# Decoder layer, attention output: twelve TensorE transposes and two ScalarE copies per step replaced by one DMA transpose

## The reference

```
_, o = jax.lax.scan(step, S0, xs)                    # per head: state 96 x 192, output 192 wide
gate = (hidden_states @ Wg).reshape(B, T, H, DV)     # H = 16, DV = 192
var = jnp.mean(o * o, axis=-1, keepdims=True)
o = o * jax.lax.rsqrt(var + EPS) * norm_weight * jax.nn.silu(gate)
return o.reshape(B, T, VAL_DIM) @ Wo                 # 3072 -> 512
```

## Time and profile before

| | |
|---|---|
| median of 3 runs | 2404.33 us (2402.9 to 2404.34) |
| profiled execution | span 2401.2 us from its first to its last instruction, no separate time is given for it |
| TensorE matmuls | 2317.9 us busy, 97% |
| VectorE | 2111.3 us, 88% |
| ScalarE | 1425.7 us, 59% |
| GpSimd | 1066.8 us, 44% |
| the 64 steps with an output | from about 120 us to 2150 us |

### The profile page before, as it was taken

The page is one execution under the profiler, slowest core; times in us unless marked ns, Lnnn a source line. Parts: engine busy times, 40 slices in busy tenths (PEclk is TensorE's granted clock), DMA queues, the critical chain, the costliest instruction groups (busy, mean ns, idle before and its releaser), DMA issues. The chain is left out here.

```text
span 2401.2 us, 55407 instructions
## 1 busy us (share of the span) xinstructions
PE 2317.9 (97%) x19896; PEld 1640.4 (68%) x19896; DVE 2111.3 (88%) x4579; ACT 1425.7 (59%) x3891; POOL 1066.8 (44%) x1543
## 2 busy tenths in 40 slices
PE   5899999999999999999999999999999999888998
PEld 3677767777777777776767777777777776773554
DVE  8999999998989999999999999999999989648776
ACT  5566666656565666666666666665555555333665
POOL 3634354444434354545343544444343535214564
PEclk8999999999999999999999999999999999788999
DMA  5211122222212112222221222221111011002000
GB/s 139 64 45 47 39 53 52 55 53 55 53 50 48 47 45 63 61 64 62 57 61 41 60 58 64 62 64 38 38 33 34 19 36 22 17 19 119 23 23 27
DMA packets 289390, 120.76 MB, mean 50 GB/s; under 512 B 211510, under 2 KB 267094, under 8 KB 288604
## 3 DMA queue, kind: packets, MB, share of 16 engines
q1 hardware_dynamic: 289116, 117.21, 18.5%
HBM read 85.42 MB, written 31.74 MB: 49 GB/s over the span
## 5 line engine op out<-in xcount | busy, mean ns | idle before, releaser
L1450 DVE SCALAR_TENSOR_TENSOR d_y<-bank,d_cw,d_y 128x508 f32<-128x508 f32 (+2 forms) x576 | 421.9, 733 | 6.3 <-ACT d_y L1205 0.8
L794 POOL TENSOR_SCALAR d_ms<-d_sso 128x4 f32<-128x4 f32 x64 | 14.5, 226 | 573.6 <-ACT d_junk L1343 573.6
L778 POOL TENSOR_TENSOR d_V<-d_tok,d_kinv 128x640 f32<-128x640 f32 (+1 forms) x128 | 130.3, 1038 | 303.8 <-issue 301.9
L1628 DVE SCALAR_TENSOR_TENSOR x<-bank,x 128x512 f32<-128x512 f32 x256 | 172.3, 677 | 51.3 <-PE bank L1018 51.3
L1205 ACT ACTIVATE d_y<-bank,d_cw 128x512 f32<-128x512 f32 x192 | 131.2, 684 | 88.6 <-PE bank L859 86.1
L1328 ACT ACTIVATE d_thg<-bank 128x384 f32<-128x384 f32 x128 | 62.2, 486 | 199.3 <-PE bank L973 196.9
L1614 DVE SCALAR_TENSOR_TENSOR d_on<-d_O,d_rn,d_gate 128x192 f32<-128x192 f32 x256 | 154.8, 663 | 0.0
L824 POOL TENSOR_SCALAR d_K<-d_tok,d_Em 128x96 f32<-128x96 f32 x256 | 151.3, 607 | 0.0
L1254 ACT ACTIVATE d_tok<-bank 128x384 f32<-128x384 f32 x256 | 125.5, 490 | 36.1 <-PE bank L875 32.1
L1212 ACT ACTIVATE d_th<-d_y 128x512 f32<-128x512 f32 x192 | 121.6, 634 | 41.3 <-DVE d_y L1456 34.8
L1471 DVE SCALAR_TENSOR_TENSOR d_yv<-d_th,d_y 128x512 f32<-128x512 f32 x128 | 98.2, 767 | 52.1 <-ACT d_th L1212 44.5
(11 more groups left out here) (341 smaller groups left out, 7115.4 us busy)
## 6 DMA issues: line engine op xcount, KB each, us to landing
lt_blocks<-d_LT SPq DMA_DIRECT2D x64, 256.0 KB, 2.4
d_fw<-turned_gate_w SPq DMA_DIRECT2D x32, 256.0 KB, 3.0
d_XT<-x_blocks SPq DMA_DIRECT2D x128, 64.0 KB, 2.3
d_X<-x_blocks SPq DMA_DIRECT2D x128, 64.0 KB, 2.3
d_fw<-turned_val_w SPq DMA_DIRECT2D x32, 256.0 KB, 3.0
d_fw<-turned_out_w SPq DMA_DIRECT2D x32, 256.0 KB, 2.8
d_st<-in_L_attn_Wg_dram SPq DMA_DIRECT2D x16, 384.0 KB, 4.2
ternary<-d_ft SPq DMA_DIRECT2D x48, 128.0 KB, 2.1
```

The costliest lines, as they stand in the source:

```text
L778: last = nc.gpsimd.tensor_tensor(V[q][:, :, lo:hi], tok[q][:, :, at:at + hi - lo], over(kinv[:, :], 2, hi - lo), ALU.mult)
L1450: nc.vector.scalar_tensor_tensor(out=yy[:, :, tap:], in0=pp[:, :, 0:P - tap], scalar=cw[:, ds(st.kp, 1), t, 3 - tap], in1=yy[:, :, tap:], ...
L1628: nc.vector.scalar_tensor_tensor(out=xs, in0=bank[(4, 7, 6, 5)[i]][:, :], scalar=1.0 / (SO * SW), in1=xs, op0=ALU.mult, op1=ALU.add).then_ ...
```

## The change

SyncE issues one DMA transpose per step that reads all twelve blocks of `ohl` in SBUF and writes them turned into `onT` in SBUF. The twelve transposes on TensorE and both copies on ScalarE are gone, with their semaphores `onT_done` and `onT_ready`; the DMA signals `onT_in` by 16. In SyncE's list the new transfer stands between the feed-forward transfers and `scatter`. It waits for `low_ready` of the step and for the product of the step before (`wo_done`). The two waits that protected PSUM banks 6 and 5 move from `turn_output` to the third and fourth batch row of `output`, and `high` and `low` wait for the DMA of the step before instead of TensorE's transposes. `onT` is laid out by batch row first. The twelve blocks are 384 KB per step.

```
-        onT = sb("onT", [P, 3, B, P], F16)
+        onT = sb("onT", [P, B, 3, P], F16)
...
+            def turn_output(st):
+
+                past(sp, "low_ready", st.n)
+                past(sp, "wo_done", B * (st.n - 1))
+                sp.dma_start_transpose(onT[:, :, :, :].rearrange("p b g t -> p (b g) t"),
+                                       ohl[:, :, :, :].rearrange("p b g t -> p (b g t)")).then_inc(s["onT_in"], 16)
...
                     gather(st)
                     for i in done_jobs(st, 0):
                         next_weights(i + 1)
+                    if st.output:
+                        turn_output(st)
                     scatter(st)
                     for i in done_jobs(st, 1):
                         next_weights(i + 1)
+                elif st.output:
+                    turn_output(st)
...
-            def turn_output(st, part):
-
-                n = st.n
-                past(pe, "low_ready", n)
-                if part == 0 and st.turn:
-                    past(pe, "LT_ready", B * n + 2 * B)
-                if part == 1 and st.recur:
-                    past(pe, "W_ready", B * n + 4)
-                for e, g in enumerate(((0, 1), (2,))[part]):
-                    for i in range(B):
-                        last = nc.tensor.transpose(bank[6 - part][:, :].bitcast(F16)[:, (e * B + i) * P:(e * B + i + 1) * P],
-                                                   ohl[:, i, g, :], idh[:, :])
-                last.then_inc(s["onT_done"], 1)
-
             def output(st, i):
 
                 n = st.n
                 if i == 0:
-                    past(pe, "onT_ready", 2 * n - 1)
+                    past(pe, "onT_in", 16 * n)
                     past(pe, "wo_ready", 2 * st.k + 2 if st.c else 2 * st.k)
+                if i == 2 and st.turn:
+                    past(pe, "LT_ready", B * n + 2 * B)
+                if i == 3 and st.recur:
+                    past(pe, "W_ready", B * n + 4)
...
-                    if i == 0 and e == 4:
-                        past(pe, "onT_ready", 2 * n)
...
-                if st.output:
-                    turn_output(st, 0)
-                    turn_output(st, 1)
                 for part in range(4 if c == 0 else 0, 6):
                     proj(2, part, 6)
...
                 def high():
                     past(a, "on_ready", B * n)
-                    past(a, "onT_done", 2 * n - 2)
+                    past(a, "onT_in", 16 * (n - 1))
...
-                def read_onT(part):
-                    past(a, "onT_done", 2 * n - 1 + part)
-                    past(a, "wo_done", B * n - B)
-                    w = (2, 1)[part]
-                    nc.scalar.activation(onT[:, 2 * part:2 * part + w, :, :].rearrange("p g b t -> p (g b t)"),
-                                         bank[6 - part][:, :].bitcast(F16)[:, 0:w * B * P], ACT.Copy).then_inc(s["onT_ready"], 1)
```

More of the change, by code:

```diff
@@ L94 @@
     gate_done gtanh_done gate_ready d_done D_ready pd_done O_ready K2_ready su_done S_ready
-    ssq_done r_ready on_ready high_ready low_ready wo_high onT_done onT_ready wo_done x_added
+    ssq_done r_ready on_ready high_ready low_ready wo_high onT_in wo_done x_added
     fw_in fw_done fsum_ready fgam_done gam_ready stat aggr set_in set_done set_read""".split()
@@ L1012, in output @@
                 wh, wl = wo[st.wn]
-                terms = [(onT[:, 0, i, :], wh[:, 0, :]), (onT[:, 0, i, :], wl[:, 0, :]), (onT[:, 1, i, :], wh[:, 1, :]),
-                         (onT[:, 1, i, :], wl[:, 1, :]), (onT[:, 2, i, :], wh[:, 0, :])]
+                terms = [(onT[:, i, 0, :], wh[:, 0, :]), (onT[:, i, 0, :], wl[:, 0, :]), (onT[:, i, 1, :], wh[:, 1, :]),
+                         (onT[:, i, 1, :], wl[:, 1, :]), (onT[:, i, 2, :], wh[:, 0, :])]
                 for e, (o, w) in enumerate(terms):
-                    if i == 0 and e == 4:
-                        past(pe, "onT_ready", 2 * n)
                     last = nc.tensor.matmul(bank[(4, 7, 6, 5)[i]][:, :], o, w, start=(e == 0), stop=(e == len(terms) - 1))
@@ L1419, in step @@
                                  (R_, copy_yj), (R_, lambda: read_qs(0)), (T_, lambda: tokens(st, 2)), (R_, join), (R_, lambda: read_qs(1)),
-                                 (T_, lambda: tokens(st, 3)), (n == NS - 1, lambda: copies(1)), (O_, lambda: read_onT(0)), (O_, lambda: read_onT(1)), (n == NS, lambda: exponential(1)),
+                                 (T_, lambda: tokens(st, 3)), (n == NS - 1, lambda: copies(1)), (n == NS, lambda: exponential(1)),
                                  (P_, lambda: tanh(st, 1)), (P_, lambda: tap0(st, 2)), (True, lambda: heads(1)), (T_, lambda: jobs(1)), (T_, norms), (R_, lambda: gate_tanh(0)),
@@ L1619, in low @@
                     v.wait_ge(s["high_ready"], n)
-                    past(v, "onT_done", 2 * n - 2)
+                    past(v, "onT_in", 16 * (n - 1))
                     flat = ohl[:, :, :, :].rearrange("p b g t -> p b (g t)")
```

## The result

The changed kernel takes 2409.05 us (median of 10 runs, 2403.53 to 2417.67) against 2403.45 us of the kernel before, measured again with it (median of 10). The ratio is 1.0032 with a 95% interval of 1.0017 to 1.0047. So it is slower, as forecast, and the time lies inside the predicted range of 2390 to 3100 us. But the predicted time was 2501 us, a loss of 97 us where 6 to 8 us were measured (by the medians and by the ratio): the forecast of the size was wrong.

What follows compares the result with a forecast made beforehand. The prediction took TensorE's own list to bound the kernel. From a 2401 us span, 57 us go, 113 us of stalls and 41 us of low clock come: 2498 us, plus 3 us to the median, 2501 us; range 2390 to 3100 us.

Steps and rivals of the forecast that it cites:

- What bounds the kernel: TensorE's list sets the length of a step; each us off it can shorten it, VectorE less than 2 us behind.
- what goes: TensorE's twelve transposes, 0.72 us in each of 64 steps, 46 us, plus 11 us of waits for ScalarE's copy: 57 us.
- what comes: Time added: TensorE's stalls waiting for the DMA transpose, 113 us, and the lowered clock behind them, 41 us.
- What each step leaves for T: Time between `low` and the product that can hide the transfer: c=1 3.5 us, c=2 4.25, c=3 4.2, c=0 1.0.
- T: Time from the end of `low` until TensorE may go on; taken as 5.0 us, ends 3.1 and 18.5.
- How long T is: T taken from the 384 KB Wg load's 4.2 us landing, plus issue and signal: 5.0 us.
- What hides it: SyncE is free then, so its new wait delays no block even at T of 12 us; TensorE has nothing to fill stalls.
- The clock: The 4.0 us stall in each c=0 step lowers TensorE's clock to 0.50, losing 2.55 us per head, 41 us.
- the faster case: Rival: T is 3.4 us and the c=0 stall leaves the clock up, giving 2385 us; chance 0.13.
- The block-by-block case: Rival: the transpose runs block by block, T far above an ordinary transfer; at T = 12, 3071 us; chance 0.27.

Runs made afterwards that it cites:

- e3_no_wait: Against the changed kernel: the DMA transposes still run, but the product with Wo reads other blocks, so TensorE does not wait for them; 2367.45 us, ratio 0.9864.

## Why the sign was right and the size wrong

- **What bounds the kernel**: right for the step with c = 2, wrong for those with c = 1 and 3. "Each us taken off that list can shorten the step" put VectorE up to 2 us behind; in the steps with c = 3 the removed 0.72 us shorten nothing, and the 57 us that I let go in full are worth 34 us where nothing is turned. The same slack gives back part of what comes: while TensorE stalls, VectorE catches up. From 130 to 1960 us TensorE's matmuls wait for the additions to x 12.1 us before, 6.8 us in the changed kernel and 25.2 us where nothing is turned. With the transfers left in and only the wait for them taken out (e3_no_wait), the kernel is 41 us faster than the changed one, while the stalls and the clock stand in the sum below with 50 + 14 = 64. So what goes and what comes are each some 23 us too large in it, with opposite signs.
- **What goes**: right as work taken off TensorE, 0.72 us per step by position on the queue; all 768 matmuls and both copies are gone. What it is worth is the point above.
- **What each step leaves for T**: right. T - 1.0 us was the forecast for the stall where c = 0, and with T = 3.8 us that is 2.8 us; measured 2.3 to 3.3 us in the steady stretch, mostly 2.7 to 2.8. For c = 1 to 3 the same rule gives 0.3 us or none with this T, and none was seen but for five slow transfers, with stalls of 0.9 to 1.1 us.
- **How long T is**: this is the step that failed. I took 5.0 us; it is 3.71 to 3.76 us in 12 of the 16 steps with c = 0 and at most 4.3 in the others. I built it from a landing time of 4.2 us, plus 0.4 to 0.5 us of issue and 0.3 us until the signal is seen. The landing time already runs from the start of the issue: the transpose lands after 3.7 us in the profile, and TensorE goes on 3.77 us after `low`. So the issue was counted twice. The 0.3 us for the signal came from setting the median landing of the block store, 2.4 us, against one store that landed after 3.0; that store's signal was seen at once, and TensorE goes on less than 0.1 us after the transpose lands. Together that is 0.8 us too much. The rest is the row that I leaned on, a load from DRAM in 4.2 us; the copy of the same size within SBUF takes 2.6 us. Two errors of 0.8 and 1.6 us in one direction met one of 1.1 us in the other, the turning with its small packets, which I had priced at nothing. Each us of T beyond 4.2 costs 64 us and each us just below it 16 to 32, so that is most of the miss: by my own formula T = 3.8 gives stalls of 0.3 + 2.8 = 3.1 us per head, 50 us, instead of 113.
- **What hides it**: right. SyncE waits for the remainder 407.5 us in all and still 723.7 us for the recursion at line 639. Nothing was late behind it.
- **The clock**: the mechanism was right, the size was not. I charged 2.55 us in each of 16 heads, 41 us; it was 1.7 us behind 8 of the 14 stalls of the steady stretch, 14 us.
- **The rivals**: the faster case needed T under 4.0 us without the clock. T was 3.8 us, but the clock took what was left: with the stall filled, the kernel is at 0.9971, faster than before. The block-by-block case is excluded by one number, 3.7 us for twelve blocks. The Trainium skill (VectorE: DVE Perf Modes, The three transpose paths) gives 1309 ns for one block by DMA. The trace does not bear out the estimate of 15.7 us that I made from it by adding twelve up; no run here moves a single block. The Trainium skill (Advanced Engine Details and Errata, X-Bar Transpose) says that a transpose is as fast as a regular DMA; measured here it is 1.1 us longer at 384 KB, 3.7 against 2.6 us.

With T and the clock as measured, the sum is 2404 - 57 + 50 + 14 = 2411 us, 2 us from the median. That it comes so close is in part luck: the 57 and the 64 are each too large by some 23 us, and the sum does not have the 13.7 us that came back in the last three steps.

## What to carry to other kernels

When work moves from a saturated engine to a transfer, compare for each kind of step the transfer's time with the work that stands between producer and consumer, and change only the steps that hide it: three of four did here, and the kernel that left the fourth alone is 1.2% faster while the plain change is 0.3% slower. Take the transfer's time from a row with the same source and destination memory, and check on one pair of rows where a landing time starts before adding anything to it. Before hoping for the whole gain, measure the floor with the work left out, and read it by kind of step: it was 34 us of 57, because in two of four steps the next engine was as close a bound.

## What the runs showed of the hardware

- The issue of a DMA transpose on SyncE takes 1.47 us for twelve 128 x 128 blocks and 1.25 us for three, against 0.51 us for a copy of the twelve. Over these two sizes it is nearly a fixed price, and its length does not delay the first packet, which starts after 1.2 us in the transpose and in the copy.
- VectorE's small instructions get longer when they meet GpSimd's. Two of 32 x 64 took 1.49 us in the kernel before at the moment when a GpSimd instruction began (first two rows), and 0.43 us in the kernel after where it began later (third and fourth row):

```profile
1016.16 1.49 DVE L1543 TENSOR_TENSOR d_prod<-d_Lb,d_XTb 32x64 f32<-32x64 f32 x2
1016.18 1.35 POOL L778 TENSOR_TENSOR d_V<-d_tok,d_kinv 128x640 f32<-128x640 f32 x1 [4.71 <-issue]
```

```profile
1024.49 0.43 DVE L1530 TENSOR_TENSOR d_prod<-d_Lb,d_XTb 32x64 f32<-32x64 f32 x2
1024.82 2.06 POOL L789 TENSOR_TENSOR d_V<-d_tok,d_kinv 128x640 f32<-128x640 f32 x2 [5.30 <-issue]
```

  The whole traces agree. In the kernel before, 213 of the 256 products of this shape ran while no GpSimd instruction did, and each took 0.24 to 0.26 us; of the 43 that overlapped one, 25 took over 0.4 us, up to 1.32. In the changed kernel 84 overlap and 65 of them take over 0.4 us, and the 256 together take 92.0 us instead of 77.1. In every kernel here that has fewer transposes on TensorE and all of VectorE's work, VectorE's busy time is up by 26 to 33 us for the same instructions (in the kernel without the remainder the two groups of products are 36 us longer than before). So a shorter TensorE list shifts such meetings; that the overlap is what lengthens the instructions was read from the traces, and no run moves GpSimd's work by itself.
- The five transfers with c > 0 in the steady stretch that landed after 5.2 to 5.4 us each had a 16 KB packet of the instruction queue starting 3.0 to 3.4 us after their issue, at the end of their own packets. Two others that met such a packet at 3.3 us landed after 3.9 us, so this is an observation and no rule.
